# Third small-head layer: the mask added to all four score banks of a step by 32x32 tiles in plain fp32, and one maximum per head

## The reference, cut to what matters

```python
q = hidden_state @ Wq + bq
k = encoder_hidden_state @ Wk + bk
v = encoder_hidden_state @ Wv + bv
scores = jnp.einsum('bkgld,bksd->bkgls', q, k) * scale
scores = scores + encoder_attention_mask[:, :, None, :, :]   # (4, 1, 256, 256)
attn = jax.nn.softmax(scores, axis=-1)
out = jnp.einsum('bkgls,bksd->bkgld', attn, v)
out = out @ Wo + bo
x = out + hidden_state                                       # then a layer norm
```

## Time and profile before

| | us |
|---|---|
| Median of three runs | 1252.83 |
| The three runs | 1250.13, 1252.83, 1253.26 |
| Span of the profiled execution, first to last instruction | 1248.4 |
| Time of the profiled execution itself | not given apart; its span is 4.4 below the median |
| Third small-head layer, from its first `by_query` to the end | 1053.5 to 1248.4 |
| PE busy | 1203.5 (96% of the span) |
| DVE busy | 888.7 (71%) |
| ACT busy | 779.8 (62%) |
| POOL busy | 598.9 (48%) |

### The profile page before, as it was taken

The page is one execution under the profiler, slowest core; times in us unless marked ns, Lnnn a source line. Parts: engine busy times, 40 slices in busy tenths (PEclk is TensorE's granted clock), DMA queues, the critical chain, the costliest instruction groups (busy, mean ns, idle before and its releaser), DMA issues.

```text
span 1248.4 us, 27144 instructions
## 1 busy us (share of the span) xinstructions
PE 1203.5 (96%) x9940; PEld 1029.8 (82%) x9940; DVE 888.7 (71%) x2304; ACT 779.8 (62%) x1889; POOL 598.9 (48%) x966
## 2 busy tenths in 40 slices
PE   8999999999999999999989899999999899999997
PEld 7999999999999999999978665786675577666664
DVE  5887877779887777778865787537788464666764
ACT  4876666668876566666874566645676654555553
POOL 3784555548875555454862443504444131324333
PEclk9999999999999999999999999999999999999999
DMA  5540100013431001001420220122222012121100
GB/s 170 153 141 31 35 26 27 27 39 107 142 100 35 27 26 35 27 27 28 126 74 27 81 81 28 51 69 74 84 68 70 10 60 64 54 70 42 40 12 18
DMA packets 56820, 75.03 MB, mean 60 GB/s; under 512 B 11312, under 2 KB 30576, under 8 KB 56688
## 3 DMA queue, kind: packets, MB, share of 16 engines
q1 hardware_dynamic: 51568, 72.75, 19.1%
q0 software_dynamic: 5120, 0.56, 0.3%
HBM read 49.46 MB, written 1.05 MB: 40 GB/s over the span
## 4 chain that ended last, share of the span: by engine, by line
PE 80%; DVE 7%; issue 5%; ACT 4%; POOL 2%; DMA 1%; ACTq 0%; DVEq 0%; POOLq 0%
PE bank L125 19%; PE bank L127 18%; PE bank L126 18%; PE bank L2052 5%; PE bank L771 4%; PE bank L1999 3%; PE bank L2009 3%; PE bank L1985 2%; PE bank L2010 2%; PE bank L1981 1%; ACT PT L2126 1%; DMA Q<-rows 1%; PE bank L178 1%; PE bank L713 1%; PE bank L1736 1%
## 5 line engine op out<-in xcount | busy, mean ns | idle before, releaser
L1095 POOL TENSOR_SCALAR E<-E,rl 128x256 f32<-128x256 f32 x256 | 243.6, 962 | 210.2 <-DVE rl L980 210.2
L2126 ACT ACTIVATE PT<-bank 128x512 f32<-128x512 f32 x320 | 173.5, 594 | 92.6 <-PE bank L2010 56.0
L846 ACT ACTIVATE QTh<-bank,bqs 128x256 fp32r<-128x256 f32 x128 | 60.8, 475 | 156.3 <-PE bank L127 156.2
L2207 DVE CUSTOM_DVE_ANT_0 Em<-bank,M 128x256 bf16<-128x256 f32 x256 | 95.1, 420 | 53.8 <-PE bank L1985 22.3
L856 ACT ACTIVATE E<-bank,nm 128x257 f32<-128x257 f32 x256 | 119.5, 481 | 1.2 <-DVE nm L950 1.0
L984 DVE TENSOR_TENSOR PTl<-bank,PTh 128x512 fp32r<-128x512 f32 x128 | 88.0, 688 | 27.3 <-ACT PTh L868 26.8
L957 DVE SCALAR_TENSOR_TENSOR QTl<-bank,bqs,QTh 128x256 fp32r<-128x256 f32 x128 | 61.6, 481 | 64.0 <-ACT KT L847 63.2
L868 ACT CAST PTh<-bank 128x512 fp32r<-128x512 f32 x128 | 75.2, 588 | 43.2 <-PE bank L771 43.2
L2201 DVE TENSOR_REDUCE nm<-bank 128x1 f32<-128x512 f32 x128 | 83.3, 685 | 23.5 <-PE bank L1981 22.3
L950 DVE TENSOR_REDUCE nm<-bank 128x1 f32<-128x257 f32 x256 | 95.5, 414 | 3.6 <-PE bank L127 3.6
L1999 PE MATMUL bank<-Q,K 51*128 51x256 f32 (+1 forms) x640 | 85.2, 315 | 4.9 <-DMA Q<-rows 2.4
(11 more groups left out here) (438 smaller groups left out, 4382.2 us busy)
## 6 DMA issues: line engine op xcount, KB each, us to landing
stage<-in_wts SPq DMA_DIRECT2D x99, 256.0 KB, 3.3
U<-in_vrows SPq DMA_DIRECT2D x64, 256.0 KB, 2.7
K<-stage SPq DMA_DIRECT2D x48, 128.0 KB
Q<-stage SPq DMA_DIRECT2D x48, 128.0 KB
K<-stage SPq DMA_DIRECT2D x48, 64.0 KB
Q<-stage SPq DMA_DIRECT2D x48, 64.0 KB
K<-xh SPq DMA_DIRECT2D x16, 128.0 KB, 3.0
Q<-rows POOLq DMA_DIRECT2D x96, 4.0 KB, 1.7
```

Source lines behind the costliest of these rows:

```text
L1095: m = pool.tensor_scalar(s.E[:, i % 3, t, 0:256], s.E[:, i % 3, t, 0:256], s.rl[:, r, t:t + 1], None, ALU.mult)
L2126: act.activation(s.PT[i % s.NPT][:, 2 * u:2 * u + 2, :].rearrange("p a b -> p (a b)"), s.STB[y][:], ACT.Exp).then_inc(S["t_ex"])
L2207: dve.tensor_tensor_reduce(out=s.Em[:, (2 * i + e) % 4], in0=bank[:, e * 256:e * 256 + 256], in1=s.M3[:, j, e, :], scale=-1.0, scalar=3.4e ...
```

## The change: what it does, and the diff

The mask is added by TensorE in both places, and in plain fp32. Four 32-row groups of one SBUF tile `MS` hold 32-row strips of the mask: groups 0 and 1 the mask as it is, groups 2 and 3 the transposed mask. In a step, after `by_query` and `by_key`, `add_masks` issues 4 x 4 matmuls with a 32x32 piece of the identity and 512 columns of mask: row group a (0 and 1 for the two `SB` banks, 2 and 3 for the two `STB` banks) and column group k (the 32 partitions of the bank). In the first five steps there are only the groups 0 and 1, in the last five only 2 and 3. `t_s` (which VectorE waits for) and `t_st` (which ScalarE waits for) are now raised by the last column group's matmuls, where `t_s` used to be raised by `by_query` itself.

VectorE takes one plain `tensor_reduce` over both query tiles instead of two custom operations. `maskparts` becomes `floor0` and `floor1`: the maximum with -3e38, in place, over half of `MS` each, in steps 10 and 12 of the batch. The mask's loads become 16 issues of 32 partitions instead of two of 128, and stand behind the 24 issues of `q_out` and `k_out` (before, ahead of them).

```diff
-TILE_COUNTS = {"s": (64, 128, 128), "mx": (64, 128, 256), "st": (64, 128, 128), "ex": (64, 128, 128),
+TILE_COUNTS = {"s": (64, 128, 128), "mx": (64, 128, 128), "st": (64, 128, 128), "ex": (64, 128, 128),
@@ IN_MLP and IN_LAYER of layer 3
-          3: {3: ["mask"], 6: ["k0", "kh", "kl"], 7: ["v0", "v1", "va", "k_out"], 8: ["maskparts"],
+          3: {2: ["mask"], 6: ["k0", "kh", "kl"], 7: ["v0", "v1", "va", "k_out"], 8: ["floor0", "floor1"],
-            3: {0: ["mask", "turn", "th", "tl", "res"], 2: ["q0"], 3: ["q1", "qh", "ql"], 5: ["k0", "kh", "kl"],
-                6: ["q_out", "k_out"], 8: ["v0", "v1", "va"], 10: ["maskparts"]}}
+            3: {0: ["turn", "th", "tl", "res"], 2: ["q0"], 3: ["q1", "qh", "ql"], 5: ["k0", "kh", "kl"],
+                6: ["q_out", "k_out"], 7: ["mask"], 8: ["v0", "v1", "va"], 10: ["floor0"], 12: ["floor1"]}}
@@ heads_prep_sp
-            w.wait_ge(S["t_mx"], s.mx((b - 1) * s.nh))
-            w.wait_ge(S["mask_low"], b - 1)
-        sp.dma_start(s.M3[:, j], dram["mask3"][b].rearrange("(t p) s -> p t s", p=128)).then_inc(S[f"ld_m3{j}"], 16)
-        sp.dma_start(s.MT[:, j], dram["mask3t"][b].rearrange("(s p) t -> p s t", p=128)).then_inc(S[f"ld_mt{j}"], 16)
+            w.wait_ge(S["t_s"], s.o["s"] + (b - 1) * s.nh)
+            w.wait_ge(S["t_st"], s.o["st"] + (b - 1) * s.nh)
+        for k in range(4):
+            for a, src in enumerate((dram["mask3"], dram["mask3"], dram["mask3t"], dram["mask3t"])):
+                rows = src[b].rearrange("(e k r) c -> k r e c", e=2, k=4)[k]
+                sp.dma_start(s.MS[j][32 * a:32 * a + 32, k, :].rearrange("r (e c) -> r e c", e=2), rows
+                             ).then_inc(S[f"ld_m3{j}"], 16)
@@ heads_prep_dve
-    if x == "maskparts":
...
+    if x in ("floor0", "floor1"):
+        w.wait_ge(S[f"ld_m3{j}"], 256 * (b // 2 + 1))
+        half = s.MS[j][:, 2 * int(x[-1]):2 * int(x[-1]) + 2, :]
+        dve.tensor_scalar(half, half, BIG, None, ALU.max).then_inc(S["mask_floor"])
@@ heads_pe
-    def add_mask(n):
...
+    def add_masks(n):
+        groups = [(y, n // s.TB, s.SB[k % len(s.SB)], "t_s") for y, k in enumerate(s.in_step(n))]
+        groups += [(2 + y, (n - s.L) // s.TB, s.STB[y], "t_st") for y, k in enumerate(s.in_step(n - s.L))]
+        w.wait_ge(S["ld_ident"], 16)
+        for k in range(4):
+            for a, b, bank, done in groups:
+                at, to = slice(32 * a, 32 * a + 32), slice(32 * k, 32 * k + 32)
+                w.wait_ge(S["mask_floor"], 2 * b + 2)
+                z = pe.matmul(bank[to, :], c.ident[at, at], s.MS[b % 2][at, k, :], start=False, stop=k == 3,
+                              skip_group_check=True)
+                if k == 3:
+                    z.then_inc(S[done])
@@ heads_dve, maxima
-        if l == 1:
+        if l != 2:
             dve.tensor_reduce(nm, bank[:].rearrange("p (a b) -> p a b", a=2), AX.X, ALU.max, negate=True
                               ).then_inc(S["t_mx"])
...
-            for e in range(2):
-                w.wait_ge(S["t_mx"], s.o["mx"] + 2 * i + e - 3)
-                dve.tensor_tensor_reduce(out=s.Em[:, (2 * i + e) % 4], in0=bank[:, e * 256:e * 256 + 256],
-                                         in1=s.M3[:, j, e, :], scale=-1.0, scalar=3.4e38, op0=ALU.add,
-                                         op1=ALU.min, accum_out=nm[:, e:e + 1]).then_inc(S["t_mx"])
```

More of the change, by code:

```diff
@@ L1247, in take_first @@
         if self.l == 3:
-            self.M3, self.MT = sb("M3", [128, 2, 2, 256]), sb("MT", [128, 2, 2, 256])
-            self.MTh, self.MTl = sb("MTh", [128, 2, 512], F32R), sb("MTl", [128, 2, 512], F32R)
+            self.MS = [sb("MS", [128, 4, 512]) for _ in range(2)]
         else:
@@ L1267, in take_rest @@
         self.rows = sb("rows", [128, 2, 128], F32R)
[L1268 to L1271, removed]
         sb = self.rest
@@ L1371, in mx @@
     def mx(self, i):
-        return self.o["mx"] + i * (1 if self.l == 1 else 2)
+        return self.o["mx"] + i * self.units
 def spread_done(c, w, l):
@@ L1653, in values @@
         z.then_inc(S[f"v{half}"])
-    if x == "maskparts":
[L1656 to L1662, removed]
-                                 op1=ALU.subtract).then_inc(S["mask_low"])
+    if x in ("floor0", "floor1"):
+        w.wait_ge(S[f"ld_m3{j}"], 256 * (b // 2 + 1))
+        half = s.MS[j][:, 2 * int(x[-1]):2 * int(x[-1]) + 2, :]
+        dve.tensor_scalar(half, half, BIG, None, ALU.max).then_inc(S["mask_floor"])
     elif x == "stats":
@@ L1978, in by_query @@
         bank = s.SB[n % len(s.SB)]
-        w.wait_ge(S["t_mx"], s.o["mx"] + (n - len(s.SB) + 1) * (2 if l == 3 else 1))
+        w.wait_ge(S["t_mx"], s.o["mx"] + n - len(s.SB) + 1)
         if l == 2:
@@ L1985, in by_query @@
             z = pe.matmul(bank[:, 256 * e:256 * e + 256], s.Q[r][at, q // s.blocks, 128 * e:128 * e + 128],
-                          s.K[r][at, q // s.rp, :], start=True, stop=True)
-        if 1 in es:
+                          s.K[r][at, q // s.rp, :], start=l != 3 or e == 0, stop=l != 3, skip_group_check=l == 3)
+        if l != 3 and 1 in es:
             z.then_inc(S["t_s"])
@@ L2002, in by_key @@
             z.then_inc(S["t_st"])
-    def add_mask(n):
-        b, bank = n // (s.WD * s.TB), s.STB[n % 2]
-        w.wait_ge(S["mask_low"], b + 1)
-        w.wait_ge(S["ident_r"], 1)
-        pe.matmul(bank[:], s.identR[:], s.MTh[:, b % 2, :], start=False, stop=False, skip_group_check=True)
-        pe.matmul(bank[:], s.identR[:], s.MTl[:, b % 2, :], start=False, stop=True, skip_group_check=True
-                  ).then_inc(S["t_st"])
+    def add_masks(n):
[10 more added lines that the diff above has]
+                    z.then_inc(S[done])
     def fours(n):
@@ L2036, in quarters @@
                 by_key(k, e)
-        for k in s.in_step(n - s.L):
-            add_mask(k)
+        add_masks(n)
     def attend(gi, k, n):
@@ L2142, in heads_act @@
     mlp_end(c, w, l - 1)
-    if l == 3:
-        w.wait_ge(S["ld_ident"], 16)
-        act.copy(s.identR[:], c.ident[:]).then_inc(S["ident_r"])
     for n in range(s.steps()):
@@ L2196, in maxima @@
         w.wait_ge(S["t_s"], s.o["s"] + n + 1)
-        if l == 1:
+        if l != 2:
             dve.tensor_reduce(nm, bank[:].rearrange("p (a b) -> p a b", a=2), AX.X, ALU.max, negate=True
                               ).then_inc(S["t_mx"])
-        elif l == 2:
+        else:
             dve.tensor_reduce(nm[:, u:u + 1], bank[:], AX.X, ALU.max, negate=True).then_inc(S["t_mx"])
-        else:
-            j = i // s.nh % 2
-            w.wait_ge(S[f"ld_m3{j}"], 16 * (i // s.nh // 2 + 1))
-            for e in range(2):
-                w.wait_ge(S["t_mx"], s.o["mx"] + 2 * i + e - 3)
-                dve.tensor_tensor_reduce(out=s.Em[:, (2 * i + e) % 4], in0=bank[:, e * 256:e * 256 + 256],
-                                         in1=s.M3[:, j, e, :], scale=-1.0, scalar=3.4e38, op0=ALU.add,
-                                         op1=ALU.min, accum_out=nm[:, e:e + 1]).then_inc(S["t_mx"])
     mlp_end(c, w, l - 1)
```

## The result

The changed kernel takes 1296.16 us (median of four runs, 1293.52 to 1298.5), the kernel before 1253.05 beside it (1250.13 to 1254.1): 1.0357 times as long, 95% interval 1.0335 to 1.0378. The profiled span grew from 1248.4 to 1292.5 us, by 44.1; 32.7 were forecast. The time lies in the predicted range, and the forecast missed by 10.7 on the median (1285.5) and by 11.4 on the span. The 4.4 us that the forecast added to the span are not all surroundings: every other execution lies 1.4 to 1.7 above its span, so the profiled one of the kernel before was itself some 3 us faster than its median.

What follows compares the result with a forecast made beforehand. Even steps were taken as bound by mask, exp and `by_key`, odd ones by TensorE's work. Terms 8.9 + 3.9 - 0.4 + 8.9 + 1.0 + 5.0 + 0.4 + 5.0 = 32.7 us on 1252.8 gave 1285.5, range 1264 to 1312.

Steps and rivals of the forecast that it cites:

- The mask on TensorE: Mask matmuls in each step: all 16 tiles overlap, last one out at 1.15 us, TensorE free after about 0.99.
- rivals with a narrower overlap: Mask matmuls: only eight tiles run at once (1309 us) or four (1445); chance 0.14 together, 0.03 for four.
- the one with halves beside each other: Mask matmuls: a small tile's two halves overlap, bank 3 out at 0.72, time 1253.7, no change; chance 0.07.
- The narrow rival: Mask matmuls eight at a time: three rounds or more, 0.43 more in each of 55 steps, +24 us, 1309.
- Even and odd steps: Plain steps: chain mask, exp, `by_key` takes 2.76 us in both kinds; even +8.9, odd +3.9, nine long ones -0.4.
- The 0.04: Plain step's chain: exp starts 0.04 us after the mask's last bank is finished, as in the kernel before.
- Maxima on VectorE: Fewer operations are worth nothing; maxima waiting for the mask delay divisions and transposes after three batches: 3.05 + 3.05 + 2.8 us.
- The 1.0 for parts of the maxima: Once in each of two batches, transposition waits for these parts behind `floor1` and the residual: 0.5 each, +1.0 us.
- First steps: Steps 0 to 4 gain eight mask tiles each: 4 x 1.03 us and 0.9 for the fifth, +5.0.
- 0.1 for the change of tiling: Steps 0 to 4: 0.1 us for changing tiling, within 1.03 us for a first step's eight tiles.
- The mask's loads and the floor: Sixteen loads at 0.48 us an issue land at 1093.1; VectorE waits at `floor0`; +5.0 us over three batches.
- The 0.7 in each of the next two batches: `floor0` after the first batch: VectorE's wait for the loads is about 1 us, the loss 0.7 each.

Runs made afterwards that it cites:

- run 1: Changed kernel with the two STB tiles issued ahead of the two SB tiles within each column group: 1294.16 us, ratio 1.0354 to the kernel before.
- run 2: Changed kernel with all eight STB tiles issued first, then the eight SB tiles: 1290.24 us, ratio 1.0329 to the kernel before.
- run 10: Kernel before, with only the STB mask done by eight small tiles, in bf16 from two parts: 1238.99 us, ratio 0.9916.
- run 7: Kernel before, with only VectorE's part: plain maxima over both query tiles, leaving out the mask: 1249.36 us, ratio 0.9999.
- run 8: Changed kernel without its SB tiles, `by_query` raising `t_s` again, mask left out of the maxima: 1321.58 us, ratio 1.0577 to the kernel before.
- run 3: Changed kernel with the mask's 16 loads ahead of the 24 Q and K issues in later batches: 1289.71 us, ratio 1.0313 to the kernel before.
- run 6: Changed kernel with STB tiles all first, mask loads ahead, and products of ones in steps without `attend`: 1287.56 us, ratio 1.0297 to the kernel before.
- run 9: Changed kernel without its SB tiles, plus products of ones in steps without `attend`: median 1319.88 us, spread too far for a ratio.
- run 4: Changed kernel with 3, later 5, products of ones on TensorE in the last steps: 1295.17 us, ratio 1.036 to the kernel before.
- run 11: Kernel before, with the STB mask by eight bf16 tiles from three parts, keeping all its bits: 1251.33 us, ratio 1.0015.

## Why the prediction was right, and where it fell short

**The mask on TensorE** was right: 1.14 for 1.15, all 16 tiles at once. The rivals with a narrower overlap fall by that row, and so does the one with halves beside each other. (The narrow rival was priced too low: 32 halves, eight at a time, are four rounds and not three, 0.86 more a step, about 1333, outside the range.) TensorE was free at 1.07, not 0.99; that is on no chain.

**Even and odd steps**: the chain was the right one, and it closes in each step. Its second term failed: "1.15 + 0.04 + 1.08 + 0.06 + 0.43". The 0.04 is 0.22. Runs 1 and 2 show why. Of the 0.18 us by which exp starts later than in run 2, about 0.07 is the two increments ahead of exp's, about 0.05 that its tile is issued eight places later, and about 0.06 that eight more tiles are in flight ahead of it. With STB's tiles all first the forecast's 2.76 is there (2.74). The mis-sized term costs 3.4 us in even steps, 3.0 in odd ones and 0.8 in the long ones: 7.2 of the 11.4 missed on the span.

For this gap the sum has only the 0.04 of the kernel before. No row of that kernel shows what several increments behind small tiles cost: of `attend`'s matmuls the last alone raises a semaphore. From the mask's last modelled end to exp the traces now show 0.22 us for the third of four increments with 16 tiles (the changed kernel), 0.14 for the first (run 1), and 0.09 for the first with eight tiles alone (its last steps).

In run 10 exp starts 0.04 after the last bf16 tile's modelled end, as before; but it waits for bank 3, whose last tile is issued four ahead of that one, so from its own tile's end it is 0.05.

**Maxima on VectorE**: right. Fewer operations are worth nothing (run 7, ratio 0.9999). Late ones cost 3.2, 3.2 and 2.9 in the four steps after the three batches (half clock taken out of the second), where the forecast had 3.05, 3.05 and 2.8. The 1.0 for parts of the maxima that come late behind `floor1` is not there: the steps around it take 2.93 like the others.

**First steps**: right, 4.92 in the layer against 5.0 (and run 8). The forecast gives no row for its 0.1 for the change of tiling. In the kernel before, the mask's first matmul, right behind the smaller scores, takes 0.51 us and its last 0.39; in the changed kernel a first step's eight tiles hold TensorE for 1.02 us (1.03 forecast). Whether the tiling makes these differences no run shows. The 0.53 ahead of the layer is less than that point moves from run to run, and nothing ties it to the change.

**The mask's loads and the floor**: the mechanism, its place and the usual price of an issue were right. The time of landing was right by luck: one slow issue added what the shorter landing took off. The stall in the first batch cost 3.4 for 3.6 forecast, and 0.9 of it is the half clock behind it, so the wait itself cost 2.6. The 0.7 in each of the next two batches is not there: VectorE waited at `floor0` once more, 0.7 us at 1146.5, and the steps behind it take as long as in run 3. Run 3's gain is larger than the term, but mixed with the clock and with the earlier stages.

**The clock** is missing from the prediction altogether. It took the full clock of the earlier trace rows as given. About 1.2 us after the second batch, 4.8 at the end and 0.9 behind `floor0`'s stall are half clock in the profiled execution. It comes with the change (3 us at half before, 22 after), in a layer where TensorE waits for exp in nearly each step and is busy 90% instead of 98%, much of it with small tiles. What exactly brings the fall is open, and so is whether the waits or the small tiles count. Ones did not hold the clock in runs 6 and 9, and run 4 does not tell; run 8, with fewer tiles at the same step time, lost it for 90 us on end; run 10, with fewer and shorter tiles but shorter steps too, kept it as the kernel before did.

The sum: 32.7, + 7.2 for the tail, + 6.0 for the clock at the end and after the second batch, + 0.5 ahead of the layer, - 0.1 in the first steps, - 0.6 after a batch apart from its clock, - 1.6 for the floor makes 44.1. The forecast was right in direction, range and main mechanism; its size was 11 short because one term was a fifth of what it is and another, the clock, was missing.

## What to carry to other kernels

In these runs nothing was ready until the second round of small tiles ended (exp started at 1.18 us at the earliest behind a plain fp32 mask of 1.09 or 1.14), and each increment ahead cost about 0.036 more, so issue first, and raise first, what the critical engine waits for. Before a mask or a bias moves to TensorE, ask which of its users is on the chain; here, in a plain step, only exp was. Tiles for that one in bf16 gained 0.8%, at the price of some bits of the mask (with all its bits, run 11, nothing was gained), while tiles for all four banks in plain fp32 lost 3.6%. And when a change leaves TensorE waiting, price its clock too (here 22 us of the layer at half instead of 3), and read the granted clock by stretch before you explain a time.

## What the runs showed of the hardware

- Sixteen 32x32 tiles, 512 columns of plain fp32 each, run as two halves each (x32) and all sixteen side by side: 1.14 us in all at full clock, 2.01 at half (changed kernel); eight take 1.09. In bf16 a round of eight tiles takes 0.22 (runs 10 and 11).
- The waiting engine starts 0.04 us after the last modelled end with one increment (kernel before) or with eight bf16 tiles (run 10), 0.09 with eight fp32 tiles, 0.14 for the first and 0.22 for the third of four increments with sixteen. From runs 1 and 2 an increment ahead costs an estimated 0.036, a tile ahead 0.01.
- Leaving out eight of sixteen tiles made the kernel some 27 us slower (run 8), with the clock at half for 172 us of the layer.
